# Attention scores of two heads per step in 64-row halves of TensorE, in a fused graph and attention block

## The chip, the cores and the metric

The kernel runs on one core of a Trainium2 chip. The metric is the device time of one execution in microseconds (us). The kernel before takes 1134.38 us, the median of 3 runs (1133.22 to 1134.51).

## The reference, cut to what matters

1250 nodes of 768 features pass a layer norm, and then a graph convolution over 20000 edges, an attention with 12 heads of 64, and a routed feed-forward with 8 experts. The change is in the attention, whose weights are a polynomial in place of the exponential:

```python
q, k, v = (qkv[0] * SCALE, qkv[1], qkv[2])
A = jnp.einsum('bhnd,bhmd->bhnm', q, k)
numerator = 1.0 + A + 0.5 * A * A
attn = numerator / numerator.sum(axis=-1, keepdims=True)
out = jnp.einsum('bhnm,bhmd->bhnd', attn, v)
```

## The kernel before

**Numbers in two parts.** TensorE multiplies in a reduced form of float32 (F32R), so each operand is split into a high part (rounded, written by ScalarE) and a low part (the rest, written by VectorE). A product of two such operands is high by high, low by high and high by low, added up in PSUM. `product` does that for 128-row operands.

**The pair loop.** The 12 heads are taken as 6 pairs, head 0 of a pair in partitions 0 to 63 and head 1 in 64 to 127. `turn(j, ...)` is one pair on each engine: 30 steps and a tail, in loops that run five times and a last turn written apart. Queries are cut into three chunks of 418, 416 and 416, keys into ten tiles of 125. Before, a step is one head, one chunk and two key tiles: steps 0 to 14 are head 0, 15 to 29 head 1, five steps to a chunk.

**A score before.** `MA` (for head 0) holds the high part of Q in the head's own 64 partitions and its low part in the other 64. K's high part `KHA` and low part `KLA` stand in both halves; the second half is a copy that SyncE's DMA queue makes (`second_half`, semaphore `k_twice`). One 128-row matmul with `KHA` then gives high by high and high by low at once, one with `KLA` the rest: two matmuls for a key tile, four for a step. `MB`, `KHB`, `KLB` are the same for head 1, split in steps 1 to 18 (`SECOND_AT`).

**A step.** TensorE writes scores into two of four banks of `ps`, ScalarE squares them (`Pf`, L824, with a bias of 1, so (1+A)^2, and adding 1 gives twice the numerator). ScalarE (L802) or VectorE (L1012) rounds that to `Ph`, VectorE writes the rest `Pl` (L1014), and three steps later (`LAG`) TensorE multiplies both by V's two parts (L1156), four matmuls. `Pf`, `Ph` and `Pl` have three places each (`RING`). At the end of a chunk `fold_out` adds the upper half of the output to the lower (ScalarE L811, VectorE L945), and `finish` multiplies by the reciprocal of the sums and splits the result (L955, L958, L959).

**Beside the steps.** TensorE also projects Q and K of the next pair, six products of 6 x 3 matmuls in slices of six (`PROJ_AT`, 18 of the steps), transposes K (`TURN_AT`) and forms a Gram matrix (`GRAM_AT`) from which the sums come in closed form (`quadratic`, `total`, `turn_inverse`, L1108, L1116, L1124). The reciprocals go through memory to be spread over partitions (`invd`, then `rden`). VectorE compares edge keys (L967, twenty per pair), and GpSimd adds edge counts to a table in memory (L363), two columns at a time. All other loads are on SyncE's queue, in the order of the code. Every order is written out by hand as step numbers in the tuples that the change edits.

**After the pairs** SyncE waits for all edge counts, loads them (`Cs`), and TensorE computes the graph convolution's product, which takes weights that the last turn splits (`load_w3`, `hi_w3` L627, `lo_w3` L633).

Of the kernel before, what the change touches and what calls it, by code (L numbers as in the profile page):

```python
# [34 lines left out]
P = 128  # L35
# [65 lines left out]
def build(nc, x, src, dst, gnn_w, gnn_b, w_qkv, b_qkv, w_proj, b_proj, sw, sb_, w1, b1, w2, b2, out,  # L101
          counts, keyd, vdram, odram, rows, x1d, invd, blank):
    ctx = ExitStack()
    with ctx:
# [14 lines left out]
        def right(stack, specs):  # L119
# [65 lines left out]
        (K32, kt2, KHA, KLA, MA, gs, Q32, OUN, R32, rden, vsb, tmpo, Pf, Ph, Pl, k1, inv, invr, KHB, KLB, MB, OHL, eqp, kcur, ccur) = region([  # L185
            ("K32", [P, N], F32), ("kt2", [P, NT, 2, P], F32R),
            ("KHA", [P, N], F32R), ("KLA", [P, N], F32R), ("MA", [P, N], F32R), ("gs", [P, 3, P], F32),
            ("Q32", [P, N], F32), ("OUN", [P, N], F32), ("R32", [P, N], F32), ("rden", [P, N], F32),
# [3 lines left out]
            ("KHB", [P, N], F32R), ("KLB", [P, N], F32R), ("MB", [P, N], F32R),  # L192
            ("OHL", [P, 2, N], F32R), ("eqp", [P, 2, WINDOW * P], BF16), ("kcur", [P, EP], F32), ("ccur", [P, EP], F32)])
        KH, KL, MQ = (KHA, KHB), (KLA, KLB), (MA, MB)
# [4 lines left out]
        qk_mm, kq_full, k_twice = sem("qk_mm"), sem("kq_full"), sem("k_twice")  # L199
        k_hi, k_lo, q_hi, q_lo = ([sem(f"{n}{a}") for a in range(2)] for n in ("k_hi", "k_lo", "q_hi", "q_lo"))  # L200
# [449 lines left out]
        def _(sp):  # L650
# [11 lines left out]
            def load_v(j, a):  # L662
                for p0, n in PARTS:
                    sp.dma_start(vsb[p0:p0 + n, :, a, :].bitcast(F32), vdram[at(j * T + p0, n), :, a * P:(a + 1) * P]
                                 ).then_inc(v_in[a], 16)

            def second_half(a, n):

                own, other = slice(a * HD, (a + 1) * HD), slice((1 - a) * HD, (2 - a) * HD)
                for done, part in ((k_hi[a], KH[a]), (k_lo[a], KL[a])):  # L670
                    sp.wait_ge(done, n)
                    sp.dma_start(part[other, :].bitcast(F32), part[own, :].bitcast(F32)).then_inc(k_twice, 16)
# [8 lines left out]
            second_half(0, 3)  # L681
# [21 lines left out]
            def turn(j, last, keyed):  # L703
                sp.wait_ge(oacc_done, 6 * j + FREE)
                load_v(j, 1)
# [3 lines left out]
                second_half(1, 3 * j + 3)  # L709
                if not last and not keyed:  # L710
                    sp.wait_ge(r_zero, 16)
                    clear(0)
                if not last:
# [32 lines left out]
        def _(act):  # L746
# [16 lines left out]
            def hi_part(a, jn, g):  # L763

                c0, w = CHUNKS[g % 3]
                h = slice(a * HD, (a + 1) * HD)
                act.wait_ge(kq_full, 6 * jn + (g + 1))
                if g < 3:
                    act.activation(KH[a][h, c0:c0 + w], K32[h, c0:c0 + w], ACT.Copy).then_inc(k_hi[a], 1)
                else:  # L770
                    act.activation(MQ[a][h, c0:c0 + w], Q32[h, c0:c0 + w], ACT.Copy).then_inc(q_hi[a], 1)
# [17 lines left out]
            for g in range(3):  # L789
                hi_part(0, 0, g)  # L790
            for g in (3, 4):
                read_kq(0, g)
            hi_part(0, 0, 3)

            def turn(j, last):
                def round_weights(i):

                    w = step(i)[4]
# [6 lines left out]
                def fold_out(s):  # L805

                    w = CHUNKS[s % 3][1]
                    act.wait_ge(pv_done, j * STEPS + (5 * s + 5))
# [9 lines left out]
                for i in range(END):  # L818
                    if i < STEPS:
                        w = step(i)[4]  # L820
# [9 lines left out]
                    if i in SECOND_AT:  # L830
                        hi_part(1, j, SECOND_AT.index(i))
                    if i in LATE_AT:
                        hi_part(0, j, 4 + LATE_AT.index(i))
                    if i % 5 == 3 and i >= 8:
                        fold_out(i // 5 - 1)
# [7 lines left out]
                    if not last:  # L843
# [3 lines left out]
                        if i in READ_AT:  # L847
                            g = READ_AT.index(i)
                            if g == 0:
                                act.wait_ge(k_lo[1], 3 * j + 3)  # L850
                                act.wait_ge(bias_ready, j + 2)
                            if g == 3:
                                act.wait_ge(r_done, 3 * j + 3)
                                act.wait_ge(q_lo[1], 3 * j + 3)
# [5 lines left out]
                        if i in FIRST_AT:  # L860
                            hi_part(0, j + 1, FIRST_AT.index(i))
# [6 lines left out]
        def _(dve):  # L868
# [8 lines left out]
            def lo_part(a, jn, g):  # L877

                own, other = slice(a * HD, (a + 1) * HD), slice((1 - a) * HD, (2 - a) * HD)
                c0, w = CHUNKS[g % 3]  # L880
                cs, n = slice(c0, c0 + w), 3 * jn + (g % 3 + 1)
                if g < 3:
                    dve.wait_ge(k_hi[a], n)
                    dve.tensor_tensor(KL[a][own, cs], K32[own, cs], KH[a][own, cs].bitcast(F32),
                                      ALU.subtract).then_inc(k_lo[a], 1)
                else:
                    dve.wait_ge(q_hi[a], n)
# [915 lines left out]
```

## Time and profile before

| | us |
|---|---|
| median of 3 runs | 1134.38 (1133.22 to 1134.51) |
| the profiled execution | 1134.08 |
| its span, first to last instruction | 1132.4 |
| span outside | 1.7 |
| TensorE busy in the span | 931.7 |
| VectorE busy | 733.0 |
| ScalarE busy | 459.4 |

The span is what the trace covers. The mean granted TensorE clock is 0.928 of full speed. Busy time of TensorE is a union of matmuls that overlap: each is shown with a duration of about twice the time from its start to the next one's. The rate is read from start to start.

### The profile page before, as it was taken

How to read it: one execution, taken by the hardware profiler on the slowest of the kernel's cores; microseconds unless marked ns; L12 is line 12 of the kernel's file. 1: busy time of each engine (PE TensorE's matmuls, PEld its weight loads, DVE VectorE, ACT ScalarE, POOL GpSimd, SP SyncE). 2: the span in 40 equal slices, each digit the busy share in tenths (PEclk: the TensorE clock that was granted, in tenths of full speed). 3: DMA queues.
4: the chain of work that ended last, by engine and by line, in shares of the span. 5: the costliest groups of instructions: out<-in, count | busy, mean ns of one | idle time of the engine just before them, and what ended most of it. 6: DMA issues, size and time to landing. Idle time of an engine off the chain costs nothing.

```text
span 1132.4 us, 15230 instructions
## 1 busy us (share of the span) xinstructions
PE 931.7 (82%) x5250; PEld 886.2 (78%) x5250; DVE 733.0 (65%) x1396; ACT 459.4 (41%) x678; POOL 308.5 (27%) x201
## 2 busy tenths in 40 slices
PE   3896789989989989989896779699999963399970
PEld 3896688888878878878885679699999963399960
DVE  6877269879889788789786445464445436166633
ACT  2311266666666666666665212110101020266520
POOL 2035555535646545533452000000000004100004
PEclk9998899999999999999998889899999975599995
DMA  9966433373363454498534564736252332879978
GB/s 279 321 180 151 85 49 61 37 137 60 62 112 60 85 88 60 89 198 197 116 54 107 72 155 104 167 80 154 77 154 78 95 110 53 238 232 278 282 192 272
DMA packets 143091, 152.24 MB, mean 134 GB/s; under 512 B 72205, under 2 KB 119926, under 8 KB 142024
## 3 DMA queue, kind: packets, MB, share of 16 engines
q1 hardware_dynamic: 114213, 137.46, 46.7%
q0 software_dynamic: 28432, 14.05, 9.8%
q8 instruction: 26, 0.43, 0.2%
q10 hardware_dynamic: 403, 0.17, 0.1%
q14 instruction: 17, 0.14, 0.0%
HBM read 105.79 MB, written 46.78 MB: 135 GB/s over the span
## 4 chain that ended last, share of the span: by engine, by line
PE 57%; DVE 15%; ACT 9%; issue 8%; DMA 7%; POOL 2%; SPq 1%; DVEq 0%; ACTq 0%; POOLq 0%
PE ps L1770 14%; PE ps L1772 13%; PE ps L1771 13%; PE ps L1156 6%; PE ps L1140 3%; ACT Ph L802 3%; PE ps L1141 3%; ACT Pf L824 2%; DVE Pl L1014 2%; DVE Ph L1012 1%; DMA rows<-oE 1%; POOL rows L1511 1%; DMA Cs<-counts 1%; PE ps L1404 1%; PE ps L1116 1%
## 5 line engine op out<-in xcount | busy, mean ns | idle before, releaser
L363 POOL DMA_INDIRECT counts<-countc,idxu x157 | 273.4, 1741 | 308.5 <-DMA counts<-countc,idxu 229.9
L1014 DVE SCALAR_TENSOR_TENSOR Pl<-Pf,Ph 125x832 fp32r<-125x832 f32 (+1 forms) x180 | 184.3, 1026 | 72.6 <-ACT Ph L802 68.5
L824 ACT ACTIVATE Pf<-ps 125x832 f32<-125x832 f32 (+1 forms) x180 | 155.8, 866 | 145.9 <-PE ps L1141 140.6
L1156 PE MATMUL ps<-Ph,vsb 125*128 125x416 f32 (+1 forms) x360 | 132.1, 367 | 9.2 <-DVE Pl L1014 8.8
L1156 PE MATMUL ps<-Pl,vsb 125*128 125x416 f32 (+1 forms) x360 | 128.0, 356 | 0.0
L1511 POOL DMA_INDIRECT rows<-XF,slots x10 | 14.8, 1480 | 341.1 <-DVE slots L1626 338.4
L1770 PE MATMUL ps<-XH,wqkH 128*128 128x416 f32 (+1 forms) x216 | 81.6, 378 | 19.9 <-DVE R L932 10.2
L1770 PE MATMUL ps<-wH,XH 128*125 128x384 f32 x240 | 84.8, 353 | 9.9 <-DVE OHL L959 5.8
L1156 PEld LDWEIGHTS ps<-Ph,vsb 125*128 125x128 f32 x360 | 68.8, 191 | 19.9 <-DVE Pl L1014 9.5
L1771 PE MATMUL ps<-wL,XH 128*125 128x384 f32 x240 | 83.3, 347 | 0.0
L1772 PE MATMUL ps<-wH,XL 128*125 128x384 f32 x240 | 82.9, 346 | 0.0
L802 ACT ACTIVATE Ph<-Pf 125x832 fp32r<-125x832 f32 (+1 forms) x90 | 80.0, 895 | 0.7
L1140 PE MATMUL ps<-MA,KHA 128*125 128x416 f32 (+1 forms) x180 | 70.2, 390 | 10.4 <-DVE MA L888 10.4
L1772 PE MATMUL ps<-XH,wqkL 128*128 128x416 f32 (+1 forms) x216 | 78.1, 361 | 0.0
L1771 PE MATMUL ps<-XL,wqkH 128*128 128x416 f32 (+1 forms) x216 | 77.9, 361 | 0.0
L1770 PE MATMUL ps<-HH,CH 125*125 125x384 f32 x200 | 69.4, 347 | 7.0 <-DVE CL L1327 7.0
L1140 PE MATMUL ps<-MB,KHB 128*125 128x416 f32 (+1 forms) x180 | 65.7, 365 | 8.7 <-ACT Pf L824 8.7
L1156 PEld LDWEIGHTS ps<-Pl,vsb 125*128 125x128 f32 x360 | 69.3, 193 | 0.9
L1771 PE MATMUL ps<-HL,CH 125*125 125x384 f32 x200 | 68.4, 342 | 0.0
L1772 PE MATMUL ps<-HH,CL 125*125 125x384 f32 x200 | 68.4, 342 | 0.0
L1141 PE MATMUL ps<-MB,KLB 128*125 128x416 f32 (+1 forms) x180 | 64.2, 357 | 0.0
L1141 PE MATMUL ps<-MA,KLA 128*125 128x416 f32 (+1 forms) x180 | 64.1, 356 | 0.0
(235 smaller groups left out, 2130.8 us busy)
## 6 DMA issues: line engine op xcount, KB each, us to landing
Cs<-counts SPq DMA_DIRECT2D x20, 546.9 KB
w1s<-L_ffn_w SPq DMA_DIRECT2D x8, 1152.0 KB, 8.6
w2s<-L_ffn_w SPq DMA_DIRECT2D x8, 1152.0 KB, 6.5
rows<-blank SPq DMA_DIRECT2D x2, 4215.0 KB
odram<-OHL SPq DMA_DIRECT2D x12, 625.0 KB, 8.9
oS<-odram SPq DMA_DIRECT2D x10, 750.0 KB, 4.8
vdram<-VS SPq DMA_DIRECT2D x10, 672.0 KB
vsb<-vdram SPq DMA_DIRECT2D x12, 560.0 KB
```

The source lines that it names most:

```text
L363: pool.indirect_dma_start(out=counts, out_offset=bass.IndirectOffsetOnAxis(ap=idxu[:, c:c + 1], axis=0), in_=countc[:, c:c + 1], in_offset ...
L802: act.activation(Ph[:, i % RING, :, 0:w], Pf[:, i % RING, :, 0:w], ACT.Identity, bias=1.0).then_inc(p_hiA, 1)
L824: act.activation(Pf[:, i % RING, :, 0:w], ps[0:T, 2 * (i % 2):2 * (i % 2) + 2, 0:w], ACT.Square, bias=1.0).then_inc(sq_done, 1)
L1012: dve.tensor_scalar(h, f, 1.0, None, ALU.add).then_inc(p_hiD, 1)
L1014: dve.scalar_tensor_tensor(out=p, in0=f, scalar=1.0, in1=h.bitcast(F32), op0=ALU.add, op1=ALU.subtract).then_inc(p_lo, 1)
L1140: pe.matmul(out_, KH[a][:, kt * T:(kt + 1) * T], q, start=True, stop=False)
L1141: ins = pe.matmul(out_, KL[a][:, kt * T:(kt + 1) * T], q, start=False, stop=True)
L1156: ins = pe.matmul(ps[:, 4 + s % 2, 0:w], vsb[:, 2 * kp + t, a, :], part[:, m % RING, t, 0:w], start=(kp == 0 and t == 0 and part is Ph), s ...
L1511: pool.indirect_dma_start(out=rows, out_offset=bass.IndirectOffsetOnAxis(ap=slots[:, i:i + 1], axis=0), in_=XF[:, i, :], in_offset=None).t ...
L1770: pe.matmul(out, lh, rh, start=(k == 0), stop=False)
L1771: pe.matmul(out, lh, rl, start=False, stop=False)
L1772: ins = pe.matmul(out, ll, rh, start=False, stop=(k == tiles - 1))
```

## The change

A step now is one chunk and one key tile for both heads; the first ten steps are chunk 0. K and Q are kept as one high and one low tile each over all 128 partitions (`KH`, `KL`, `QH`, `QL`), head 0 in the lower 64 and head 1 in the upper 64. A score is three matmuls of 64 rows for each head, alternating between the heads, into two banks: six matmuls in place of four. The copies of K in the other half are gone, with their four DMAs per pair, and so is `SECOND_AT`: there are six high parts and six low parts per pair where there were twelve of each, over 128 partitions in place of 64.

The output of a chunk is now in banks 4 and 5, one for each head, for all ten steps of the chunk. The next chunk needs both banks, so both are folded at one place (`FOLD_AT`), and the first V product of chunks 1 and 2 comes one step later, next to the second (`PV_AT`). V is loaded by halves of the key tiles for both heads, in place of by head. Two of the three `finish` calls move from steps 30 and 32 to 21 and 27. K's parts of the next pair move from steps 24, 25, 26 to 25, 27, 30. In the last turn two of three weight loads stand at the front of SyncE's queue, ahead of the store and load of the reciprocals.

```diff
+        FIRST_AT = (25, 27, 30, 28)
         LATE_AT = (2, 5)
-        SECOND_AT = (1, 3, 6, 9, 13, 18)
-        FIRST_AT = (24, 25, 26, 28)
-        FINISH_AT = (30, 32, END - 1)
+        FINISH_AT = (21, 27, END - 1)
+        FOLD_AT = (13, 23, 33)
+        PV_AT = [m + LAG + (m in (10, 20)) for m in range(STEPS)]
...
-            a, c, kp = i // 15, (i // 5) % 3, i % 5
-            return a, c, kp, CHUNKS[c][0], CHUNKS[c][1]
+            c, kt = i // 10, i % 10
+            return c, kt, CHUNKS[c][0], CHUNKS[c][1]
+
+        def keys_for(kt):
+            return 1 + max(g for g in range(3) if CHUNKS[g][0] < (kt + 1) * T)
...
             def turn(j, last, keyed):
-                sp.wait_ge(oacc_done, 6 * j + FREE)
-                load_v(j, 1)
                 if not last:
                     sp.wait_ge(wqk_lo, 2 * j + 3)
                     load_w(j + 2, 1)
-                second_half(1, 3 * j + 3)
...
                     store_inverse(j)
-                    sp.wait_ge(pv_done, j * STEPS + STEPS // 2)
+                    load_inverse(j)
+                    sp.wait_ge(pv_done, j * STEPS + 25)
                     load_v(j + 1, 0)
-                    load_inverse(j)
                     if not keyed:
                         clear(1)
-                    second_half(0, 3 * j + 6)
+                    sp.wait_ge(pv_done, j * STEPS + STEPS)
+                    load_v(j + 1, 1)
                     if keyed:
                         load_pair_keys(j + 1)
                 else:
+                    sp.wait_ge(g_mm, PAIRS)
+                    sp.wait_ge(k_lo, 3 * PAIRS)
+                    load_w3(sp, 3)
+                    load_w3(sp, 4)
                     store_inverse(j)
                     load_inverse(j)
-                    sp.wait_ge(g_mm, PAIRS)
-                    for wc in (3, 4, 5):
-                        load_w3(sp, wc)
+                    load_w3(sp, 5)
...
-                        for t in range(2):
-                            kt = 2 * kp + t
-                            out_ = ps[0:T, 2 * (i % 2) + t, 0:w]
-                            q = MQ[a][:, c0:c0 + w]
-                            pe.matmul(out_, KH[a][:, kt * T:(kt + 1) * T], q, start=True, stop=False)
-                            ins = pe.matmul(out_, KL[a][:, kt * T:(kt + 1) * T], q, start=False, stop=True)
+                        for n, (k_, q_) in enumerate(((KH, QH), (KL, QH), (KH, QL))):
+                            for a in range(2):
+                                h = slice(a * HD, (a + 1) * HD)
+                                ins = pe.matmul(ps[0:T, 2 * (i % 2) + a, 0:w], k_[h, kt * T:(kt + 1) * T],
+                                                q_[h, c0:c0 + w], start=(n == 0), stop=(n == 2))
                         ins.then_inc(sc_done, 1)
```

Three places of the order. The first is TensorE at step 5 of the first turn. In the kernel before this step begins a new chunk of head 0; `q_lo0` is the semaphore of the low part of Q, `sq_done` that of the square, `p_lo` that of `Pl`.

```order
L1133 REGISTER_ALU
L1135 REGISTER_ALU [waits q_lo0]
L1140 MATMUL ps<-MA,KHA 125x416 [waits sq_done]
L1141 MATMUL ps<-MA,KLA 125x416
L1140 MATMUL ps<-MA,KHA 125x416
L1141 MATMUL ps<-MA,KLA 125x416
L1156 MATMUL ps<-Ph,vsb 128x418 [waits p_lo]
L1156 MATMUL ps<-Pl,vsb 128x418
```

The same place of the changed kernel, steps 6 and 7 of the first turn (rows with x2 are two matmuls, one for each head):

```order
L1126 REGISTER_ALU [waits k_lo]
L1130 MATMUL ps<-QH,KH 125x418 [waits sq_done]
L1130 MATMUL ps<-QH,KH 125x418
L1130 MATMUL ps<-QH,KL 125x418 x2
L1130 MATMUL ps<-QL,KH 125x418 x2
L1146 MATMUL ps<-Ph,vsb 128x418 [waits p_lo]
L1146 MATMUL ps<-Pl,vsb 128x418
```

Four 128-row matmuls became six of 64 rows between the same V products, and the wait for a part of Q in the middle of the first ten steps became waits for parts of K.

The second place is VectorE in steps 2 to 4, before; `KLB` is the low part of K of head 1, `MA` receives the low part of Q of head 0, `R` is the closed-form sum that the projections of step 7 wait for.

```order
L884 TENSOR_TENSOR KLB<-K,KHB 64x418 [waits k_hi1]
L1011 ISA
L1012 TENSOR_SCALAR Ph<-Pf 125x836 [waits sq_done]
L1014 SCALAR_TENSOR_TENSOR Pl<-Pf,Ph 125x836 [waits p_hiD]
L887 REGISTER_ALU
L888 TENSOR_TENSOR MA<-Q,MA 64x416 [waits q_hi0]
L1007 REGISTER_ALU
L1009 REGISTER_ALU [waits pv_done]
L1014 SCALAR_TENSOR_TENSOR Pl<-Pf,Ph 125x836 [waits p_hiA]
L884 TENSOR_TENSOR KLB<-K,KHB 64x416 [waits k_hi1]
L932 SCALAR_TENSOR_TENSOR R<-ps,k,Q 128x418 [waits gq_mm]
```

The same steps of the changed kernel:

```order
L1006 ISA
L1007 TENSOR_SCALAR Ph<-Pf 125x836 [waits sq_done]
L1009 SCALAR_TENSOR_TENSOR Pl<-Pf,Ph 125x836 [waits p_hiD]
L880 ISA
L881 TENSOR_TENSOR QL<-Q,QH 128x416 [waits q_hi]
L1002 REGISTER_ALU
L1004 REGISTER_ALU [waits pv_done]
L1009 SCALAR_TENSOR_TENSOR Pl<-Pf,Ph 125x836 [waits p_hiA]
L923 REGISTER_ALU
L924 SCALAR_TENSOR_TENSOR R<-ps,k,Q 128x418 [waits gq_mm]
```

The two parts of `KLB` are gone from between the steps' own work.

The third place is TensorE at step 14 of the changed kernel, where the second chunk's first V product follows the fold of both banks (`oacc_done`):

```order
L1130 MATMUL ps<-QH,KH 125x416 [waits sq_done]
L1130 MATMUL ps<-QH,KH 125x416
L1130 MATMUL ps<-QH,KL 125x416 x2
L1130 MATMUL ps<-QL,KH 125x416 x2
L1142 REGISTER_ALU
L1146 MATMUL ps<-Ph,vsb 128x416 [waits p_lo,oacc_done]
L1146 MATMUL ps<-Pl,vsb 128x416
L1146 MATMUL ps<-Ph,vsb 128x416
L1146 MATMUL ps<-Pl,vsb 128x416
L1146 MATMUL ps<-Ph,vsb 128x416 [waits p_lo]
```

Step 13 has no V product, and step 14 has two.

## Rows read from the trace of the kernel before

**Rows 1.** ScalarE's timeline: start, length, the first square of turns 2 and 3.

```profile
307.37 0.87 ACT L824 ACTIVATE Pf<-ps 125x836 f32<-125x836 f32 x1 [2.85 <-PE ps L1141]
...
390.04 0.87 ACT L824 ACTIVATE Pf<-ps 125x836 f32<-125x836 f32 x1 [2.93 <-PE ps L1141]
```

**Rows 2.** Busy times by window of turn 2: length, engines, clock, DMA share, GB/s.

```profile
307.40:321.00 13.60, 12.18 (x61) 11.01 (x60) 10.78 (x16) 10.38 (x15) 6.02 (x4) 1.00 0.96 191
...
357.00:380.00 23.00, 23.00 (x125) 22.27 (x124) 19.67 (x37) 15.79 (x26) 13.86 (x9) 1.00 0.37 48
380.00:390.00 10.00, 7.45 (x42) 6.69 (x42) 8.44 (x18) 3.90 (x7) 5.95 (x4) 1.00 0.31 32
sum 82.60, PE 75.17 PEld 70.05 DVE 70.16 ACT 53.58 POOL 45.67; mean PE 15.03 PEld 14.01 DVE 14.03 ACT 10.72 POOL 9.13
```

**Rows 3.** TensorE's timeline in steps 12 and 13 of turn 2: start, duration.

```profile
339.67 0.43 PE L1156 MATMUL ps<-Ph,vsb 125*128 125x416 f32 x1
339.94 0.35 PE L1156 MATMUL ps<-Pl,vsb 125*128 125x416 f32 x1
...
340.51 0.49 PE L1116 MATMUL ps<-blocks,R 128*125 128x2 f32 x4
340.87 0.43 PE L1770 MATMUL ps<-XH,wqkH 128*128 128x416 f32 x1
...
342.09 0.35 PE L1140 MATMUL ps<-MA,KHA 128*125 128x416 f32 x1
342.28 0.35 PE L1141 MATMUL ps<-MA,KLA 128*125 128x416 f32 x1
```

**Rows 4.** TensorE's timeline after the 20-column transpose of step 16.

```profile
349.54 0.45 PE L1140 MATMUL ps<-MB,KHB 128*125 128x418 f32 x1
349.82 0.35 PE L1141 MATMUL ps<-MB,KLB 128*125 128x418 f32 x1
```

**Rows 5.** Waits in turn 2 (307 to 389 us): total us, times, longest.

```profile
PE ps L1770 <- DVE R L932: 2.1, 1, 2.1
...
PE ps L1140 <- DVE MA L888: 1.4, 1, 1.4
```

**Rows 6.** Groups of turn 2, VectorE: busy us, mean ns, idle before.

```profile
L959 DVE SCALAR_TENSOR_TENSOR OHL<-R,bcols,OHL 128x416 fp32r<-128x416 f32 x2 | 1.3, 652 | 0.1
...
L888 DVE TENSOR_TENSOR MB<-Q,MB 64x416 fp32r<-64x416 f32 x2 | 1.2, 589 | 0.1
...
L955 DVE TENSOR_TENSOR R<-OUN,rden 128x416 f32<-128x416 f32 x2 | 1.2, 586 | 0.0
...
L958 DVE TENSOR_SCALAR OHL<-R,bcols 128x416 fp32r<-128x416 f32 x2 | 0.9, 439 | 0.1
```

**Rows 7.** Groups of turn 2, ScalarE: the same columns.

```profile
L769 ACT ACTIVATE KHB<-K 64x416 fp32r<-64x416 f32 x2 | 1.1, 549 | 0.0
```

**Rows 8.** DMA issues of turn 2: size each, median us to landing.

```profile
kt<-keyd SPq DMA_DIRECT2D x2, 1280.0 KB, 6.0
...
rden<-invd SPq DMA_DIRECT2D x2, 312.5 KB, 5.7
```

**Rows 9.** Waits in the last turn (557 to 640 us).

```profile
PE ps L1140 <- ACT Pf L824: 8.7, 1, 8.7
ACT wH L627 <- DMA wst<-L_gnn_W: 8.1, 1, 8.1
```

**Rows 10.** SyncE's timeline after the pairs: the counts' loads.

```profile
597.76 16.03 SPq L621 DMA_DIRECT2D wst<-L_gnn_W  x3
...
642.51 18.01 SPq L98 DMA_DIRECT2D Cs<-counts  x6
```

**Rows 11.** All instructions of L363, the edge counts: ns, first and last start; waits.

```profile
L363 POOL DMA_INDIRECT counts<-countc,idxu x157: 1550/1606/2480, 68.9 to 608.1; - x157
...
  DMA counts<-countc,idxu: 229.9, 77
...
  DVE idxu L985: 3.7, 1
```

More of the change, by code:

```diff
@@ L660, in load_w, with load_v @@
                              ).then_inc(wqk_in[s_], 16)
-            def load_v(j, a):
+            def load_v(j, h):
                 for p0, n in PARTS:
[L664 to L672, printed above, removed]
+                    sp.dma_start(vsb[p0:p0 + n, 5 * h:5 * h + 5].rearrange("p i a d -> p i (a d)").bitcast(F32),
+                                 vdram[at(j * T + p0, n), 5 * h:5 * h + 5, :]).then_inc(v_in[h], 16)
             sp.sem_inc(ohl_free, FREE)
@@ L680, in _ @@
             load_v(0, 0)
-            second_half(0, 3)
+            load_v(0, 1)
             def store_inverse(j):
@@ L708, in turn @@
                     load_w(j + 2, 1)
-                second_half(1, 3 * j + 3)
[L710 to L713, printed above, removed]
+                    if not keyed:
+                        sp.wait_ge(r_zero, 16)
+                        clear(0)
                     sp.wait_ge(wqk_lo, 2 * j + 4)
@@ L818, in turn @@
                 for i in range(END):
+                    if i in FOLD_AT:
+                        fold_out(2 * FOLD_AT.index(i))
+                        fold_out(2 * FOLD_AT.index(i) + 1)
                     if i < STEPS:
-                        w = step(i)[4]
+                        w = step(i)[3]
                         act.wait_ge(sc_done, j * STEPS + (i + 1))
@@ L875, in pair_bias, with lo_part @@
                                   ALU.mult).then_inc(bias_ready, 1)
-            def lo_part(a, jn, g):
-                own, other = slice(a * HD, (a + 1) * HD), slice((1 - a) * HD, (2 - a) * HD)
+            def lo_part(jn, g):
                 c0, w = CHUNKS[g % 3]
@@ L1128, in turn @@
                     if i < STEPS:
-                        a, c, kp, c0, w = step(i)
-                        if i % 15 == 0:
-                            pe.wait_ge(k_twice, 64 * j + 32 * (a + 1))
-                        if i % 5 == 0:
-                            pe.wait_ge(q_lo[a], 3 * j + (c + 1))
+                        c, kt, c0, w = step(i)
+                        if i == 0 or i < 10 and keys_for(kt) > keys_for(kt - 1):
+                            pe.wait_ge(k_lo, 3 * j + keys_for(kt))
@@ L1152, in turn @@
+                        ins.then_inc(sc_done, 1)
+                    for m in range(STEPS):
+                        if PV_AT[m] != i:
+                            continue
+                        c, kt, c0, w = step(m)
+                        if m in (0, 5):
+                            pe.wait_ge(v_in[m // 5], MOVED * j + MOVED)
+                        if m == 0:
                             pe.wait_ge(oacc_done, 6 * j + FREE)
+                        elif kt == 0:
+                            pe.wait_ge(oacc_done, 6 * j + (2 * c + FREE))
@@ L1153, in turn @@
                         pe.wait_ge(p_lo, j * STEPS + (m + 1))
-                        for t in range(2):
+                        for a in range(2):
                             for part in (Ph, Pl):
-                                ins = pe.matmul(ps[:, 4 + s % 2, 0:w], vsb[:, 2 * kp + t, a, :],
-                                                part[:, m % RING, t, 0:w], start=(kp == 0 and t == 0 and part is Ph),
-                                                stop=(kp == 4 and t == 1 and part is Pl))
+                                ins = pe.matmul(ps[:, 4 + a, 0:w], vsb[:, kt, a, :], part[:, m % RING, a, 0:w],
+                                                start=(kt == 0 and part is Ph), stop=(kt == 9 and part is Pl))
```

86 lines of the change are left out of this document (36 added, 50 removed).

## The prediction

> **What bounds the kernel now.** I began with ScalarE's timeline, because its squares mark the steps. The first squares of turns 2 and 3 stand 82.67 us apart [rows 1], so a turn takes about 82.6 us, and six of them are some 44% of the kernel. Then I read the windows of one turn [rows 2]. TensorE is busy 75.2 of 82.6 us, VectorE 70.2, ScalarE 53.6. So TensorE bounds and VectorE is close behind. The windows differ: from 357 to 380 us, where projections run, TensorE is busy all 23.0 us and VectorE 19.7; in the first 13.6 us TensorE has 1.4 idle, and in the last 10 us 2.6. Over the turn it is idle 82.6 - 75.2 = 7.4 us.
>
> The waits of the turn say for whom [rows 5]: once 2.1 us for `R` of VectorE (the projections of step 7), once 1.4 us for the low part of Q in `MA` (step 5). Both stand behind a VectorE that is busy 10.8 of the first 13.6 us, and part of that work is what the change removes.
>
> TensorE's timeline gives the price of a product. Two 416-column matmuls in a stream start 0.19 us apart (342.09 and 342.28) [rows 3], though each is shown as 0.35 long. A step's four score matmuls cost 0.76 us, the V products as much, and a slice of a projection six, 1.14 us: 2.66 us in a step that has all three.
>
> After the turns comes one place more. In the last turn TensorE waits 8.7 us for a square, while ScalarE waits 8.1 us for a weight load [rows 9], which SyncE issued only at 597.8 us, after the reciprocals [rows 10]. And GpSimd's edge counts go on until 608.1 us plus one landing [rows 11]; their loads start at 642.5 [rows 10].
>
> **The scores, the term that decides.** Six matmuls of 64 rows replace four of 128. No row of before has a 64-row matmul, so the cost is bounded from both sides. From below: the two heads' matmuls sit in different halves of the rows, and if the halves work at the same time, three pairs at 0.19 make 0.57 us, 0.19 less than now. The weight loads don't forbid that, but nearly: four matmuls of only two columns, each with its own weights of 125 columns, take 340.51 to 340.87, 0.09 us each [rows 3], so six loads need 0.54 us. From above, with nothing overlapped: 6 x 0.19 = 1.14 us. Entering a half-row mode and leaving it happens twice a step. When TensorE starts after a stall, its weights not yet loaded, the second matmul comes 0.27 us after the first (339.67 and 339.94 [rows 3]), 0.08 more than in a stream; behind the 20-column transpose, which uses the array in another width, 0.28 (349.54 and 349.82 [rows 4]). So a change of mode that costs only a bare weight load is 0.08 to 0.09 us, and 0.57 + 2 x 0.08 = 0.73. If one of the two is hidden, it is 0.65. I take 0.70, between these: 0.06 us less than now. It counts where TensorE bounds, the 18 steps with a projection slice: 18 x 0.06 = 1.1 us a turn. The bounds are 18 x 0.19 = 3.4 us won, and the rivals below.
>
> The Trainium skill (TensorE: Matmul & The Clock Gate, Part 3) says that a matmul of few rows takes as long as a full one, and that matmuls in different row groups run at the same time, which speaks for the overlap, with 3.07 times the rate for four tiles of 32 rows. No row here shows it. By an estimate from that page, two halves would run at about 1.5 to 2 times the rate of one, 0.57 to 0.76 us for the six.
>
> **VectorE and ScalarE.** Twelve low parts become six, each as long as before: 0.589 us for 64 partitions [rows 6], and an operation on 128 partitions with the same columns, L955, takes 0.586 [rows 6]. So VectorE has 6 x 0.59 = 3.5 us less a turn, ScalarE 6 x 0.55 = 3.3 us [rows 7]. Three of the removed low parts stand in steps 1, 3 and 6, ahead of what TensorE waits for. The wait for `MA` at step 5 (1.4) goes, since chunk 1 of Q is first read at step 10. `R` comes up to 3 x 0.59 = 1.8 us sooner, which would take most of the 2.1. Together at most 3.2; the same removals serve both waits, so I take 2.5.
>
> **The end of a turn.** Two `finish` calls, 0.59 + 0.44 + 0.65 = 1.68 us each [rows 6], leave steps 30 and 32, where they stand ahead of the last low part of the transposed K, and so of the Gram matrix. TensorE idles 2.6 us there [rows 2]. In their place stands the third part of K, 0.59. I take 1.2 us won, between nothing and the 2.6.
>
> **What this costs elsewhere.** The two calls go to steps 21 and 27. VectorE had 23.0 - 19.7 = 3.3 us free from 357 to 380 [rows 2], and gets 2 x 1.68 = 3.4. It becomes the bound there or ties. Also, the call at 21 reads `rden`, which lands 5.7 us after its issue [rows 8]. What is queued behind that wait on VectorE is `Pl`, on which V products wait. I take 1.0 us lost, between nothing and 3.4.
>
> The double folds cost the same work at three places in place of six. Behind the last V product of a chunk TensorE has a set of scores and a slice (0.70 + 1.14), then scores again (0.70), 2.5 us, before it wants the banks; the two copies of ScalarE and two additions of VectorE need about four operations of 0.5 to 0.6, overlapped by two, 1.8 us. Nothing is lost, and if the cover went, it would be under 1 us a place. The new V loads are issued after V product 25 and after the last, each some eight steps of at least 1.46 us, 11 us, before their first use; `rden`, of about the size of one, lands in 5.7 us [rows 8]. The keys' load (6.0 us to landing [rows 8]) is queued behind the second, and VectorE first reads it in step 5, behind three steps of 0.70 + 1.14 and two of 1.46, 8.4 us. I take both at nothing; if the V load ahead delays the keys by its whole 5.7, VectorE waits 3 us a turn. The four copies by DMA leave the queue; nothing waited for them.
>
> **The last turn.** Its weight loads stand at the front, so the 8.1 us wait of ScalarE goes, and with it 8 of TensorE's 8.7.
>
> **The sum.** Five turns at 1.1 + 2.5 + 1.2 - 1.0 = 3.8 make 19.0. The last turn has no projections and no next pair: 2.5. The weights: 8.0. Together 29.5 us. One floor stands behind it. The counts' loads wait for the last edge count, at about 608.1 + 6 = 614 us; its chain of 77 waits for its own DMAs [rows 11] does not depend on the turns, save for 3.7 us of waiting for indices that come earlier now. The loads would be issued at 642.5 - 29.5 = 613.0, so this floor takes at most 1 or 2 us: I take 1. 1134.08 - 29.5 + 1.0 = 1105.6, in the profiled execution's own time, which is 0.3 under the median. Predicted: 1106 us.
>
> **The rivals.**
>
> (A) Each change of mode waits until the matmuls in flight are out. A matmul is shown 0.35 long but starts 0.19 after its neighbour, so 0.16 is in flight, and with the bare weight load 0.25 a change: 0.57 + 0.50 = 1.07 us a step, 0.31 more than now in all 30 steps, 9.3 us a turn. The remaining idle time absorbs half of 3.7. Net: 75.2 + 9.3 + 1.9 = 86.4, 3.8 more a turn, 23 in all, less 8 for the weights: 1149 us. It decides from the point where the other gains, 2.7 a turn and 8 / 6 = 1.3 from the weights, are eaten: 4.0 / 30 = 0.13 over 0.76, so at 0.89 us for a step's scores, 0.16 for a change. For it speaks that TensorE had only few such changes before; against it the 0.28 of [rows 4], which is no more than a bare load. The Trainium skill (TensorEngine Tiling (Array Packing), Key Properties) has this rule: changing the tiling mode, not just the tile, drains TensorE; the trace, as far as one transpose can show it, does not agree.
>
> (B) The halves do not overlap: 1.14 us a step, 0.38 more, 11.4 us a turn. 75.2 + 11.4 + 1.9 = 88.5, 5.9 more, 35 in all, less 8: 1161 us.
>
> (C) The scores gain nothing, and VectorE takes over: waits for `rden` at step 21 and a full VectorE until 28 give back what the first steps won. One us a turn, 5, with 2 and 8 of the last turn: 15 us, 1119. The near tie in the 357 to 380 window speaks for it.
>
> **How the numbers follow.** Forecast 0.64, (A) 0.13, (B) 0.11, (C) 0.12. With the scores at their lower bound, 0.57, the turns win 2.3 us more each, 1094 us, where the floor of the edge counts would begin to hold; this is the low end. The high end reaches to (A), 1148, and leaves (B) and part of (A) out. Within 0.2% is 2.3 us, about what a measurement of this kernel can tell from none. Faster: the forecast and (C), 0.76. Same: a part of (A) near its turning point, 0.04. Slower: 0.20.
>
> **What the profile would show.** Right: matmuls of the two heads start much less than 0.19 us apart, and from the first of a step's scores to the first V product is 0.65 to 0.75 us; the step with a projection slice is 2.6 us; a turn is near 79 us; no wait of ScalarE for weights in the last turn; the counts' loads are issued at about 614. Wrong: the six start 0.19 apart (B), or a gap of 0.2 or more stands at each passage from 64 to 128 rows (A), or VectorE waits for `rden` and TensorE for `Pl` in steps 21 to 28 (C).

## The result, and the profile after

The changed kernel takes 1142.75 us (median of 15 runs, 1138.9 to 1147.72), the kernel before beside it 1135.75 (15 runs, 1132.68 to 1139.6): a ratio of 1.0064, 95% interval 1.0047 to 1.0081. It is slower by 7 us (0.6%), where 1106 was forecast; the time lies inside the range, near its upper end.

The page of the changed kernel (busy us, share of the span, instructions) against 1132.4 us of span before:

```profile
span 1139.2 us, 15818 instructions
...
PE 958.2 (84%) x5610; PEld 838.1 (74%) x5610; DVE 707.0 (62%) x1360; ACT 434.7 (38%) x642; POOL 305.1 (27%) x201
```

ScalarE's timeline of it shows where turns 2 and 3 begin, as [rows 1] does for before, and the windows show a whole turn and then 17 us of it:

```profile
313.46 0.87 ACT L820 ACTIVATE Pf<-ps 125x836 f32<-125x836 f32 x1 [0.95 <-PE ps L1130]
...
400.15 0.87 ACT L820 ACTIVATE Pf<-ps 125x836 f32<-125x836 f32 x1 [0.95 <-PE ps L1130]
```

```profile
313.40:400.10 86.70, 80.50 (x458) 62.73 (x456) 66.50 (x130) 49.41 (x72) 48.84 (x28) 0.98 0.39 61
```

```profile
375.00:392.00 17.00, 17.00 (x92) 14.28 (x91) 11.12 (x19) 10.44 (x16) 10.41 (x7) 0.92 0.30 38
```

This turn takes 86.7 us in place of 82.67. VectorE fell from 70.2 to 66.5 us busy and ScalarE from 53.6 to 49.4, 3.7 and 4.2, where 3.5 and 3.3 were reckoned. TensorE rose from 75.2 to 80.5. Over the first five turns (first square of the first turn to first square of the last) the time is 573.88 - 140.78 = 433.1 us; before it was 557.06 - 140.73 = 416.3. The last turn, first to last square, fell from 69.6 to 62.4 us. What follows the last square takes 502.9 us in place of 505.7. Together 16.8 - 7.1 - 2.8 = 6.9 us more, the difference of the spans.

TensorE's timeline in two steps of turn 2 (start, duration; x2 is two matmuls that the view lists together, one for each head) shows the first cause:

```profile
354.01 0.35 PE L1761 MATMUL ps<-XH,wqkL 128*128 128x416 f32 x1
354.30 0.46 PE L1130 MATMUL ps<-QH,KH 64*125 64x416 f32 x2
354.58 0.35 PE L1130 MATMUL ps<-QH,KL 64*125 64x416 f32 x2
354.77 0.35 PE L1130 MATMUL ps<-QL,KH 64*125 64x416 f32 x2
355.05 0.46 PE L1146 MATMUL ps<-Ph,vsb 125*128 125x416 f32 x1
355.35 0.35 PE L1146 MATMUL ps<-Pl,vsb 125*128 125x416 f32 x1
```

The six score matmuls go as three pairs, 0.19 us apart: the two halves of the rows do work at the same time, and six cost the time of three. But each passage between 128 and 64 rows takes 0.20 us beyond the stream. Going in, 354.01 to 354.30 is 0.29 and 354.30 to 354.58 is 0.28, where both would be 0.19. Going out, 354.77 to 355.05 is 0.28 and 355.05 to 355.35 is 0.30. So half of the price stands ahead of the first matmul in the new mode and half behind it. From 354.01 to 355.35 are 1.34 us where five starts of 0.19 would make 0.95: 0.39 for the two passages. A step's scores cost 0.57 + 0.39 = 0.96 us, 0.20 more than before. Steps without a projection slice show it too, scores of one to scores of the next (356.12 and 357.83) 1.71 us in place of 1.52.

The weight loads say what is lost. Their timeline, same step:

```profile
354.29 0.18 PEld L1130 LDWEIGHTS ps<-QH,KH 64*125 64x125 f32 x2 [0.28 <-issue]
354.40 0.19 PEld L1130 LDWEIGHTS ps<-QH,KL 64*125 64x125 f32 x2
354.59 0.19 PEld L1130 LDWEIGHTS ps<-QL,KH 64*125 64x125 f32 x2
355.05 0.19 PEld L1146 LDWEIGHTS ps<-Ph,vsb 125*128 125x128 f32 x1 [0.27 <-issue]
```

In the stream a load starts some 0.18 us ahead of its matmul (354.40 for 354.58) and is hidden. At both passages it starts with its matmul (355.05), after 0.27 to 0.28 us without a load. So the first load of the new mode starts only 0.07 us before the shown end of the last matmul of the old one (354.01 + 0.35 = 354.36), and is not hidden. The Trainium skill (TensorEngine Tiling (Array Packing), Key Properties) says that changing the tiling mode drains TensorE. The trace agrees in that each change costs 0.20 us; whether the array is quite empty then it doesn't show, since the ends of matmuls are modelled. Nor do the runs separate the wait ahead of the load from the load itself.

The second cause stands at the double fold. VectorE's timeline before TensorE's eight V products of step 24, and TensorE's beside it:

```profile
369.92 1.02 DVE L1009 SCALAR_TENSOR_TENSOR Pl<-Pf,Ph 125x832 fp32r<-125x832 f32 x1 [1.63 <-ACT Ph L795]
370.86 0.58 DVE L947 TENSOR_TENSOR R<-OUN,rden 128x418 f32<-128x418 f32 x1
371.61 0.44 DVE L950 TENSOR_SCALAR OHL<-R,bcols 128x418 fp32r<-128x418 f32 x1 [0.16 <-DVE R L947]
372.08 0.65 DVE L951 SCALAR_TENSOR_TENSOR OHL<-R,bcols,OHL 128x418 fp32r<-128x418 f32 x1
372.65 0.48 DVE L959 SCALAR_TENSOR_TENSOR eqp<-kt,kcur,triw 128x256 bf16<-128x256 f32 x1
373.06 0.08 DVE L959 DVE_READ_ACCUMULATOR eqp<-kt,kcur,triw 128x1 f32 x1
373.17 1.20 DVE L937 TENSOR_TENSOR OUN<-ps,tmpo 64x416 f32<-64x416 f32 x2
```

```profile
371.20 0.35 PE L1130 MATMUL ps<-QL,KH 64*125 64x416 f32 x2
374.43 0.71 PE L1146 MATMUL ps<-Ph,vsb 125*128 125x416 f32 x1 [2.87 <-DVE OUN L937]
374.94 0.55 PE L1146 MATMUL ps<-Pl,vsb 125*128 125x416 f32 x1
375.29 0.55 PE L1146 MATMUL ps<-Ph,vsb 125*128 125x416 f32 x1
```

The `finish` of step 21 did not wait for `rden`; it stands with its three operations and one compare ahead of the two additions of the fold (L937), 2.3 us from 370.86. TensorE waits 2.87 us for them, and then its matmuls start 0.35 us apart in place of 0.19 until 377.7: they run at 1.2 in place of 2.4 GHz (the window from 375 to 392 us above has a mean granted clock of 0.92). Nine matmuls at 0.16 more are 1.4 us beside the 2.87.

The waits of TensorE in turn 2, against [rows 5]:

```profile
PE ps L1146 <- DVE OUN L937: 2.9, 1, 2.9
...
PE ps L1759 <- DVE R L924: 1.8, 1, 1.8
```

The 1.4 us for `MA` are gone, the 2.1 for `R` only fell to 1.8. And behind the turns (SyncE's timeline, and the edge counts, against [rows 10, 11]):

```profile
652.30 10.62 SPq L98 DMA_DIRECT2D Cs<-counts  x4
```

```profile
L361 POOL DMA_INDIRECT counts<-countc,idxu x157: 1551/1568/2522, 71.2 to 626.4; - x157
```

The counts' loads are issued 9.8 us later than before, behind the turns; the last edge count started 26 us ahead of that, so that floor was not reached. But that last edge count itself started 18 us later than before (626.4 for 608.1), although the prediction held that its chain does not depend on the turns.

### The profile page after: what moved, and what is told of

The parts are those of the page before. It is cut to its first block, busy times and chain, and to the rows that moved or that the text cites. A ratio compares the mean times of both kernels' runs of the same rounds, so it can differ in the third digit from the quotient of the medians.

```text
span 1139.2 us, 15818 instructions
## 1 busy us (share of the span) xinstructions
PE 958.2 (84%) x5610; PEld 838.1 (74%) x5610; DVE 707.0 (62%) x1360; ACT 434.7 (38%) x642; POOL 305.1 (27%) x201
## 4 chain that ended last, share of the span: by engine, by line
PE 56%; DVE 19%; issue 9%; DMA 8%; ACT 5%; POOL 2%; SPq 1%; DVEq 0%; ACTq 0%; POOLq 0%
PE ps L1759 12%; PE ps L1761 12%; PE ps L1760 12%; PE ps L1146 8%; PE ps L1130 7%; ACT Ph L795 3%; DVE Pl L1009 2%; DVE eqs L487 2%; DMA vdram<-VS 2%; DVE Ph L1007 2%; DVE eqp L959 2%; DMA rows<-oE 1%; POOL rows L1500 1%; PE ps L1393 1%; DMA rows<-XF,slots 1%
## 5 line engine op out<-in xcount | busy, mean ns | idle before, releaser
L361 POOL DMA_INDIRECT counts<-countc,idxu x157 | 270.3, 1722 | 329.0 <-DMA counts<-countc,idxu 227.1
L1146 PE MATMUL ps<-Ph,vsb 125*128 125x416 f32 (+1 forms) x360 | 148.3, 412 | 22.0 <-DVE OUN L937 19.0
L1146 PE MATMUL ps<-Pl,vsb 125*128 125x416 f32 (+1 forms) x360 | 131.4, 365 | 0.0
L1759 PE MATMUL ps<-XH,wqkH 128*128 128x416 f32 (+1 forms) x216 | 84.0, 389 | 18.1 <-DVE wqkL L866 8.3
L1759 PE MATMUL ps<-wH,XH 128*125 128x384 f32 x240 | 84.8, 353 | 8.0 <-DVE wL L454 4.1
L1130 PE MATMUL ps<-QH,KH 64*125 64x416 f32 (+1 forms) x360 | 81.6, 450 | 1.9 <-DVE QL L881 1.9
L1130 PEld LDWEIGHTS ps<-QH,KH 64*125 64x125 f32 x360 | 33.3, 181 | 49.2 <-issue 44.5
L1130 PE MATMUL ps<-QH,KL 64*125 64x416 f32 (+1 forms) x360 | 63.8, 351 | 0.0
L1130 PE MATMUL ps<-QL,KH 64*125 64x416 f32 (+1 forms) x360 | 63.7, 349 | 0.0
```

The costliest lines, as they stand in the source:

```text
L361: pool.indirect_dma_start(out=counts, out_offset=bass.IndirectOffsetOnAxis(ap=idxu[:, c:c + 1], axis=0), in_=countc[:, c:c + 1], in_offset ...
L1130: ins = pe.matmul(ps[0:T, 2 * (i % 2) + a, 0:w], k_[h, kt * T:(kt + 1) * T], q_[h, c0:c0 + w], start=(n == 0), stop=(n == 2))
L1146: ins = pe.matmul(ps[:, 4 + a, 0:w], vsb[:, kt, a, :], part[:, m % RING, a, 0:w], start=(kt == 0 and part is Ph), stop=(kt == 9 and part i ...
L1759: pe.matmul(out, lh, rh, start=(k == 0), stop=False)
```

## The experiments

**The finish late again.** The first run undoes one part:

```diff
-        FINISH_AT = (21, 27, END - 1)
+        FINISH_AT = (30, 32, END - 1)
```

> The changed kernel with the finish calls back at steps 30, 32 and 35. Theory: the call at step 21 stands on VectorE ahead of the fold at step 22, so TensorE waits 2.9 us for OUN once a turn and its clock then falls to half for some 4 us. Without it the 19 us of OUN waits go, the clock stays whole, and the step from 24 to 25 falls from 6.3 to 8.9 us to about 3.7; less 1 us a turn for the calls at the end: 1142 - 19 - 8 + 6 = about 1121 us. Rival (the passages between 64 and 128 rows alone cost what was lost): the wait moves elsewhere and the time stays within 3 us of 1142.

Measured: 1129.41 us (10 runs; before 1133.45), ratio 0.9959 (0.9935 to 0.9984). Against the changed kernel's 1.0064 this is 1.0% or 12 us less. The wait at step 24 falls to 1.16 us, and no half-speed matmuls follow:

```profile
370.78 0.46 PE L1146 MATMUL ps<-Ph,vsb 125*128 125x416 f32 x1 [1.16 <-DVE OUN L937]
```

From the square of step 24 to that of step 25 it is 4.5 us in place of 6.3 to 8.9. The place of two calls decides the sign of the whole change. Both were moved together, so what the call at step 27 cost by itself is not known. The gain is less than was expected for two reasons. The waits for `OUN` fell from 19.0 us in all to 8.7 and not to nothing: the double fold alone still costs 1.2 us a turn. And the calls at steps 30 and 32 lengthen the end of the turn again by 1.35 us, not 1 (10.65 us from the last square to the next turn's first, in place of 9.3).

**The whole rows: no passages.** Three 128-row matmuls in place of six of 64 rows. Here the scores of both heads are added together, so this leaves out their separation.

```diff
-                            for a in range(2):
-                                h = slice(a * HD, (a + 1) * HD)
-                                ins = pe.matmul(ps[0:T, 2 * (i % 2) + a, 0:w], k_[h, kt * T:(kt + 1) * T],
-                                                q_[h, c0:c0 + w], start=(n == 0), stop=(n == 2))
+                            ins = pe.matmul(ps[0:T, 2 * (i % 2) + n % 2, 0:w], k_[:, kt * T:(kt + 1) * T],
+                                            q_[:, c0:c0 + w], start=(n < 2), stop=(n > 0))
```

> The changed kernel with the three score products over all 128 rows, one matmul each, into the same two banks; this leaves out the separation of the heads and so changes the scores' values. It has as many columns to stream as three overlapped pairs but no passage to another mode. Theory (a passage costs about 0.2 us, two a step): a step with a slice falls from 2.86 to 2.47 us, one without from 1.72 towards 1.5, where ScalarE and VectorE bound; the turn loses 6 to 8 us, 1142 - 42 = 1100 us. Rival (the pairs of 64-row matmuls themselves are slower than one full matmul): also faster, but the gaps before the first score and before the first V product would stay.

Measured: 1110.06 us (one run), 33 less than the changed kernel. With the finish late as well:

> The three full-row products (which leave out the separation of the heads) with the finish calls back at 30, 32 and 35: e1 without any passage between 64 and 128 rows. Theory: 0.39 us a step less than e1 wherever TensorE bounds; the turn falls from 84.5 to about 78 us, 1129 - 38 = 1091 us. Rival (the passages are covered elsewhere by VectorE's work): a turn of 82 or more.

Measured: 1103.9 us (one run), 25 less than with the six of 64 rows. TensorE's timeline of it, from one step's scores to the next:

```profile
348.02 0.35 PE L1759 MATMUL ps<-XH,wqkL 128*128 128x416 f32 x1
348.21 0.35 PE L1128 MATMUL ps<-QH,KH 128*125 128x416 f32 x1
...
348.60 0.35 PE L1128 MATMUL ps<-QL,KH 128*125 128x416 f32 x1
348.79 0.35 PE L1144 MATMUL ps<-Ph,vsb 125*128 125x416 f32 x1
...
350.68 0.35 PE L1128 MATMUL ps<-QH,KH 128*125 128x416 f32 x1
```

The order of the steps, the waits and the banks are the same, and no gap is left on either side of the scores, so it was the change between 64 and 128 rows that made them. The step with a slice is 2.47 us, as 13 starts of 0.19 make it. The expected size was missed: 30 steps x 0.39 = 11.7 us a turn should go from TensorE's work, and the five turns (first square of the first to first square of the last, as above) became shorter by 5.1 each, (425.9 - 400.5) / 5. In turn 2 TensorE is busy 9.2 us less, but idle 3.5 us more: it waits 2.4 us for `R`, 1.8 for `Pl` and 1.8 for `OUN`. So the passages cost as much as if 13 of the 30 steps were bound by TensorE to the full, where the prediction had counted 18.

**Head by head.** To see whether the overlap needs the alternation (with the finish late):

```diff
-                        for n, (k_, q_) in enumerate(((KH, QH), (KL, QH), (KH, QL))):
-                            for a in range(2):
+                        for a in range(2):
+                            for n, (k_, q_) in enumerate(((KH, QH), (KL, QH), (KH, QL))):
```

> e1 with the same six 64-row matmuls of a step in another order, the three of head 0 and then the three of head 1. Theory (neighbours of different halves run at the same time, those of the same half do not): only one neighbouring pair overlaps, so a step's scores take five times 0.19 in place of three, 0.38 us more; in steps where TensorE bounds that is 7 to 11 us a turn, 1129 + 50 to 65, about 1185 us. Rival (TensorE finds the other half's matmul by itself, whatever the order): within 5 us of 1129.

Measured: 1134.12 us (one run), a span of 1132.4 against 1130.1 with the alternation, and five turns of 425.0 us against 425.9. The theory fell. TensorE's timeline of this kernel still shows three pairs:

```profile
345.63 0.46 PE L1130 MATMUL ps<-QH,KH 64*125 64x416 f32 x2
345.92 0.36 PE L1130 MATMUL ps<-QH,KL 64*125 64x416 f32 x2
346.11 0.35 PE L1130 MATMUL ps<-QL,KH 64*125 64x416 f32 x2
346.40 0.46 PE L1146 MATMUL ps<-Ph,vsb 125*128 125x416 f32 x1
```

From 345.63 to 346.40 is 0.77 us, as with alternation (354.30 to 355.05, 0.75). The view doesn't tell which head a matmul is of, so how the three of head 1 come beside those of head 0 stays open. That three behind each other can overlap with the three after them is what the time shows.

**Half as many passages.** TensorE takes two steps together (with the finish late): scores of both, then the V products of both, then the rest.

```diff
-                for i in range(STEPS + LAG + 1):
+                def scores(i):
...
+                def values(i):
...
+                def beside(i):
...
+                for i in range(0, STEPS + LAG + 1, 2):
+                    for do in (scores, values, beside):
+                        for i_ in (i, i + 1):
+                            do(i_)
```

> e1 with TensorE's rows of two steps put together: scores of steps i and i+1, then the V products of both, then the rest of both. Half as many passages. Theory (0.2 us a passage): 30 fewer a turn, of which those where TensorE bounds count, 4 to 5 us a turn, 25 us under e1: about 1098 us. Rival (the pipeline needs a step at a time: ScalarE and VectorE are starved by the lumps): no gain over e1, or slower.

Measured: 1112.5 us (1110.85 to 1115.61), ratio 0.9828 (0.9793 to 0.9863), 17 us less than with the finish late alone. The six starts of scores have one way in and one way out:

```profile
328.33 0.35 PE L1770 MATMUL ps<-XH,wqkL 128*128 128x418 f32 x1
328.61 0.46 PE L1130 MATMUL ps<-QH,KH 64*125 64x416 f32 x2
328.90 0.35 PE L1130 MATMUL ps<-QH,KL 64*125 64x416 f32 x2
...
329.66 0.35 PE L1130 MATMUL ps<-QL,KH 64*125 64x416 f32 x2
329.94 0.46 PE L1148 MATMUL ps<-Ph,vsb 125*128 125x418 f32 x1
330.23 0.35 PE L1148 MATMUL ps<-Pl,vsb 125*128 125x418 f32 x1
```

That is 15 ways there and back less, 5.9 us of a turn, and 3.2 shorter turns, (425.9 - 410.0) / 5. It gave 17 us of the 35 that the price alone would. The rest went into longer waits: for `Pl` 9.4 us in the five turns in place of 1.2, and for `R` 11.6 in place of 7.9, with half-speed matmuls behind it:

```profile
319.71 0.69 PE L1768 MATMUL ps<-XH,wqkH 128*128 128x418 f32 x1 [2.33 <-DVE R L924]
320.20 0.55 PE L1769 MATMUL ps<-XL,wqkH 128*128 128x418 f32 x1
320.55 0.55 PE L1770 MATMUL ps<-XH,wqkL 128*128 128x418 f32 x1
```

Moving the two calls of `finish` once more, now to steps 24 and 28, gained nothing:

```diff
-        FINISH_AT = (30, 32, END - 1)
+        FINISH_AT = (24, 28, END - 1)
```

> e7 with the first two finish calls at steps 24 and 28, behind the fold at 22 and not ahead of it. Theory (what hurt was the place ahead of the fold, not the early finish): no OUN waits come back and the end of the turn is 1 us shorter, 5 us under e7, about 1107 us. Rival (VectorE is full from 24 to 28 and Pl comes late): 1112 or more.

Measured: 1112.69 us (1111.82 to 1114.38), ratio 0.981 (0.9787 to 0.9833). The waits for `OUN` did not come back (1.0 us in five turns), so that part of the theory held. But the end of a turn stayed at 10.5 us, and the gain expected there didn't come.

**Twice as many passages.** The order in a step becomes: first pair of scores, V products of head 0, the other two pairs, V products of head 1 (finish late, one step at a time).

```diff
-                        for n, (k_, q_) in enumerate(((KH, QH), (KL, QH), (KH, QL))):
-                            for a in range(2):
...
+                        pair(i, 0)
...
                         for a in range(2):
+                            if a == 1 and i < STEPS and m == PV_AT.index(i):
+                                pair(i, 1)
+                                pair(i, 2)
                             for part in (Ph, Pl):
```

> The kernel with the late finish, with the order of TensorE's matmuls inside a step changed: first pair of score halves, V products of head 0, second and third pair, V products of head 1. The same matmuls, but four passages between 64 and 128 rows in a step where there were two. Theory (each passage costs TensorE 0.20 us, as the gaps of 0.28 and 0.30 us beside the 0.08 to 0.10 of a weight load suggest): 0.39 us more in the 27 steps of a turn that have both kinds, 10.5 us a turn, 63 us in all, 1192 us. If what the pairs of steps gave back is the true price on the path (17 us for 90 round trips less, 0.19 each): 31 us, 1160 us. Rival (a passage costs nothing beyond the weight load, and the gain of the pairs of steps came from fewer waits of TensorE for the other engines): 1130 to 1135 us, with the matmuls 0.19 us apart across the passage.

Measured: 1209.23 us (one run), 80 more than with the finish late. TensorE's timeline of a step with four passages:

```profile
378.06 0.45 PE L1123 MATMUL ps<-QH,KH 64*125 64x416 f32 x2
378.45 0.46 PE L1154 MATMUL ps<-Ph,vsb 125*128 125x416 f32 x1
378.75 0.35 PE L1154 MATMUL ps<-Pl,vsb 125*128 125x416 f32 x1
379.03 0.45 PE L1123 MATMUL ps<-QH,KL 64*125 64x416 f32 x2
379.32 0.35 PE L1123 MATMUL ps<-QL,KH 64*125 64x416 f32 x2
379.60 0.46 PE L1154 MATMUL ps<-Ph,vsb 125*128 125x416 f32 x1
...
380.19 0.45 PE L1123 MATMUL ps<-QH,KH 64*125 64x416 f32 x2
```

The step is 380.19 - 378.06 = 2.13 us: seven starts of 0.19 are 1.33, and four passages of 0.20 make the rest. The five turns are 10.4 us longer each, (477.7 - 425.9) / 5, where 10.5 were expected. The expectation counted 27 steps with two more passages; in the code they are 25, since steps 13 and 23 have no V product either, and 25 x 0.39 = 9.8 us. Here the added passages count about in full. The last turn became 24 us longer, not 10, for another reason. TensorE waits 0.96 us there, at 651 us, and from then on runs at half clock:

```profile
656.00:680.00 24.00, 24.00 (x70) 11.86 (x68) 11.72 (x16) 8.28 (x10) 8.44 (x5) 0.50 0.21 29
```

It is shown busy for all of these 24 us at a granted clock of 0.50, with no wait in them.

**The weights of the last turn.** First the changed kernel with its weight loads back behind the reciprocals, then the kernel before with two of the three loads ahead of them, and nothing else changed. The diff is that of the second; the first is its reverse:

```diff
                 else:
+                    sp.wait_ge(g_mm, PAIRS)
+                    sp.wait_ge(k_lo[1], 3 * PAIRS)
+                    load_w3(sp, 3)
+                    load_w3(sp, 4)
...
                     store_inverse(j)
                     load_inverse(j)
-                    sp.wait_ge(g_mm, PAIRS)
-                    for wc in (3, 4, 5):
-                        load_w3(sp, wc)
+                    load_w3(sp, 5)
```

> The changed kernel with the last turn's three weight loads behind the reciprocals' store and load again. Theory (the early loads were worth what was forecast): 8 us slower, 1150. Rival (in the changed kernel other waits of the last turn cover the load): within 2 us of 1142.

Measured: 1151.31 us (1147.8 to 1151.83), ratio 1.0153 (1.0116 to 1.0191), 8.6 us more than the changed kernel by the medians, 10 by the ratios. The wait is back:

```profile
ACT wH L629 <- DMA wst<-L_gnn_W: 7.8, 1, 7.8
```

> The kernel before with one part of the change alone: in the last turn the loads of two weight parts stand ahead of the reciprocals' store and load (they wait for the second low part of K). Theory (this part is independent of the scores): the 8.1 us wait for weights goes and the time falls by 8 us, to about 1125. Rival (a load that early delays another, or the end of the turns is set by the edge counts): under 3 us.

Measured: 1126.33 us (1125.92 to 1126.56) beside 1134.9 of before, ratio 0.9927 (0.9907 to 0.9947). So this move alone makes the kernel before 8.6 us faster, much as it does the changed one. It is also the fair kernel to compare with: beside it the changed kernel loses some 16 us and not 7, and the one with the finish late (1129.41) is 3 us behind, which the two intervals do not separate. Of the kernels that compute everything, only those with two steps together are faster than it.

**R first.** From the kernel with two steps together, VectorE's `quadratic` goes ahead of the compares of its step, and the first four compares go to step 9.

```diff
-        COMPARE_AT = (6, 7, 7, 8, 10, 10, 11, 12, 13, 14, 15, 15, 16, 17, 17, 18, 20, 20, 21, 22)
+        COMPARE_AT = (9, 9, 9, 9, 10, 10, 11, 12, 13, 14, 15, 15, 16, 17, 17, 18, 20, 20, 21, 22)
...
+                    if i - 1 in QUAD_AT:
+                        quadratic(QUAD_AT.index(i - 1))
                     if not last:
...
-                    if i - 1 in QUAD_AT:
-                        quadratic(QUAD_AT.index(i - 1))
```

> The kernel with TensorE's rows of two steps together, with VectorE's R (quadratic) ahead of the key compares and of the low parts of its step, and the four earliest compares moved to step 9. In the trace without this the product of step 6 waits 2.3 us for R in turns 2 to 5 (less in the first turn, which has fewer of them ahead) and TensorE then runs ten matmuls at half the granted clock. Theory (that wait and the clock after it are what a turn beyond the first pays): 1.5 to 2 us less a turn, 1104 us (1100 to 1108). Rival (the wait is set by TensorE's own chain from the scores over ScalarE, so R comes no sooner, or the compares push the low parts at step 9 by as much): 1112 us, within 0.2%.

Measured: 1108.92 us (1106.12 to 1109.4), ratio 0.9762 (0.9728 to 0.9796), the fastest kernel here that computes everything. The wait fell only from 2.33 to 1.92 us, by one compare, and half-speed matmuls still follow it. The kernel is 3.6 us faster than with two steps together by the medians and 7 by the ratios, whose intervals just touch. So the theory was right in direction; of the 8 us expected, half to nearly all came.

## Why the prediction was wrong

- **What bounds the kernel** was right: TensorE's time went up, and the kernel with it, although VectorE and ScalarE had each some 4 us less to do in a turn.
- **The halves overlap** was right: three pairs 0.19 us apart. (B), 1161 us, is out.
- **The scores at 0.70 us: this is the step that failed.** The term "a change of mode that costs only a bare weight load is 0.08 to 0.09 us" measured 0.20, so a step's scores cost 0.96 in place of 0.70, and not 0.06 us less than before but 0.20 more. That is past the 0.89 at which (A) decides. The 0.28 of [rows 4] was misread. It is the gap behind the first matmul after the change, and that part was 0.09 here too; the other 0.10 stands ahead of that matmul, where [rows 4] show nothing. The matmul ahead of it in the same view is the transpose:

```profile
349.45 0.28 PE L1124 MATMUL ps<-ident,inv 125*20 125x125 f32 x1 [0.33 <-DVE inv L940]
```

The next one starts 0.09 us behind it. So this neighbour, with 20 columns but over all rows, showed no cost ahead, and could not stand for a change between 64 and 128 rows. Of a turn, passages were in the sum at 18 x 0.13 = 2.3 us, and cost 5.1.
- **(A)** named the mechanism. Its price was 0.25 for a change, 1149 us; measured are 0.20 and 1142.75. That the two times lie so near is partly luck: with 0.20, its own sum gives 75.2 + 30 x 0.20 + 1.9 = 83.1 us a turn, 3 us more in all, less 8, or 1129 us, which is what the kernel with the finish late takes; the rest of the 1142.75 is what the early finish cost. Four readings of the price agree: the gaps of the timeline (0.39 for two), the step with four passages (2.13 us), the turns of that kernel (10.4 us), and the step without any (2.47 with a slice, against 2.86).
- **The finish at 21 and 27** was the second error. It was priced at 1.0 us a turn by VectorE's load over a window, against 1.2 won at the end. What it cost came from its place: it stands ahead of the fold that step 24 waits for, 2.87 us and 1.4 more at half clock, where 1.16 us of waiting would be left. Undoing both moves of the calls gave 12 us over six turns, so the terms "1.2 - 1.0", 0.2 won a turn, should have been some 2 lost. (C), which put the loss on `rden`, was wrong in its cause: VectorE didn't wait for it.
- **The double fold** was put at nothing ("Nothing is lost"). The profile shows no wait for `OUN` in turn 2 of the kernel before; with the finish late there is one of 1.2 us in each turn. The sentence also left out the `finish` call that the change puts ahead of the fold.
- **VectorE's relief, 2.5 us a turn**, gave 1.4 + 0.3 = 1.7 in the two waits. The wait for `MA` went as said. `R` came hardly sooner, though the low parts ahead of it were gone: its wait is 1.8, and one compare still stands between. What of its chain follows TensorE's own, slower steps was not separated.
- **The end of a turn** went from 10.05 to 9.3 us, 0.75 in place of 1.2.
- **The last turn's weights: 8 us**, measured 8.6 (10 by the ratios) and 8.6 in two experiments.
- **The floor of the edge counts** was not reached in any run: the counts' loads always follow the last square by 15.5 to 16.0 us. But that the chain does not depend on the turns was wrong. Its last count starts at 608.1 us before, at 626.4 in the changed kernel, at 667.9 with the passages doubled and at 596.5 without any. What it waits for beside its own DMAs was not looked into.

Of a turn, the prediction said 3.8 us less, and it was 3.4 more (16.8 / 5). The runs divide these 7.2 us in three. The five turns take 416.3 us before, 400.5 with whole rows and the finish late, 425.9 with the passages added to that, and 433.1 with the finish early as well: 3.2 us less a turn, 5.1 more and 1.4 more. In the same terms the forecast was 5.9 less (18 x 0.19 + 2.5), 2.3 more and 0.2 less. So 2.8 us of the error are the passages and 1.6 the finish (2 by the medians). The other 2.7 are the gain without passages, which came at about half its size: fewer steps are bound by TensorE than 18, and in turn 2 of that kernel TensorE waits 2.4 us for `R` (2.1 before) and 1.8 for `OUN` (none before). How these share the 2.7 is not shown. Single turns of one kernel differ by up to 3 us (84.8 to 87.9 in the changed one), so these parts are rough. The last turn, where 2.5 + 8 us were forecast, became 7.1 shorter. Why the part behind the last square took 2.8 us less stays open (it varies between 502 and 506 us in the other kernels, without a pattern).

## What to carry to other kernels

Split rows buy an overlap but each way in and out has a price, here 0.20 us, so gather all matmuls of a mode before changing it; one product saved at 0.19 doesn't pay for two passages. When a change has several parts, run each alone: here the weights' move hid half of what the scores and the finish lost. To price such a passage from a trace, measure from the last start in the old mode to the second start in the new one. And a call that is moved into a window with room has to be looked up in the order: what counts is which waited-for instruction it now stands ahead of.

## What the runs showed of the hardware

Matmuls of 64 rows in the two halves overlap whether the heads alternate or come three and three (0.75 and 0.77 us for a step's scores). The clock's answer to a wait was not the same each time: behind the wait of 2.06 us at 325.05 us of the kernel before it stayed at full speed, while with two steps together it fell behind 2.33 us, and with `R` first behind 1.92. In the kernel with doubled passages it fell after 0.96 us and stayed at half for over 24 us of a TensorE without waits; at that clock a passage cost about 0.29 us: from the last start in the old mode to the first in the new one 0.48 (656.63 to 657.11), and 0.51 to the second (657.62), where the stream has 0.35 each. Which of TensorE's doings kept the clock low in that turn and not in the others wasn't tried.
